# Second-norm rows and routed-tile rows: transposed by the DMA queue of SyncE instead of TensorE

## The reference

```
x = x + layernorm(attn(layernorm(x)))
x = x + layernorm(moe(layernorm(x)))

attn:  q, k, v = x @ Wqkv.T + b, 32 heads of 8;  a = q k^T;  ctx = a v      # no softmax: ctx = q (k^T v)
       group norm of ctx over (head feature, token), scaled by gn_w, gn_b;  ctx @ out_w.T + out_b
moe:   _ffn(x, gw, uw, dw) = (silu(x @ gw.T) * (x @ uw.T)) @ dw.T           # 256 -> 704 -> 256
       shared = _ffn(x, shared weights);  probs = softmax(x @ gate_w.T) over 8 experts
       the two largest probs per token, normalised, weigh the outputs of those two experts
       result = shared + sum over the two experts
```

## Time and profile before

| | us |
|---|---|
| median of 3 runs | 890.43 (889.81 to 890.58) |
| profiled execution, whole time | 889.43 |
| profiled execution, span | 887.7 |
| PE busy | 808.9 (91%) |
| DVE busy | 609.6 (69%) |
| ACT busy | 502.4 (57%) |
| POOL busy | 286.2 (32%) |

### The profile page before, as it was taken

One profiled execution on the slowest core, in us unless ns is written; L12 is line 12 of the kernel. 1 busy time (PEld: TensorE's weight loads), 2 busy tenths in 40 slices (PEclk: granted clock), 3 DMA queues, 4 the chain that ended last, 5 costly groups with the idle time before them and its releaser, 6 DMA issues.

```text
span 887.7 us, 21669 instructions
## 1 busy us (share of the span) xinstructions
PE 808.9 (91%) x6857; PEld 662.8 (75%) x6858; DVE 609.6 (69%) x1634; ACT 502.4 (57%) x1111; POOL 286.2 (32%) x316
## 2 busy tenths in 40 slices
PE   2689999999999999567999999999999999999990
PEld 1347777767777777455788989999899899999980
DVE  7556888887979797896787555555565565556562
ACT  1444748484847475523667555565656565656561
POOL 3010010101010100062354455555555454545432
PEclk9889999999999999879999999999999999999995
DMA  4104142423233323501133333334342434353523
GB/s 184 48 31 166 61 160 75 146 84 137 85 137 91 149 69 118 169 3 50 28 52 73 68 49 51 73 50 119 46 115 48 114 47 119 48 119 43 121 25 89
DMA packets 47061, 76.74 MB, mean 86 GB/s; under 512 B 8257, under 2 KB 38721, under 8 KB 45825
## 3 DMA queue, kind: packets, MB, share of 16 engines
q1 hardware_dynamic: 32016, 55.07, 18.0%
q0 software_dynamic: 14976, 20.78, 14.8%
HBM read 48.70 MB, written 27.39 MB: 86 GB/s over the span
## 4 chain that ended last, share of the span: by engine, by line
PE 82%; DVE 11%; issue 2%; DMA 2%; ACT 2%; POOL 1%; ACTq 0%; DVEq 0%; POOLq 0%
PE ps L829 41%; PE ps L844 20%; PE ps L900 5%; PE ps L935 4%; PE ps L894 3%; PE ps L988 2%; PE ps L912 2%; PE ps L920 2%; PE ps L870 1%; DVE hf L1143 1%; PE ps L905 1%; DVE wdn L1440 1%; DMA acc_d<-ysb,gst 1%; PE ps L939 1%; DVE hT L1153 1%
## 5 line engine op out<-in xcount | busy, mean ns | idle before, releaser
L829 PE MATMUL ps<-xhl,wgu 128*128 128x256 f16 x3630 | 449.3, 274 | 7.5 <-DVE hf L1143 5.9
L829 PEld LDWEIGHTS ps<-xhl,wgu 128*128 (+1 forms) x3630 | 353.2, 98 | 59.3 <-issue 7.6
L1143 DVE SCALAR_TENSOR_TENSOR hf<-ps,sc,silu 128x256 f32<-128x256 f32 x330 | 159.4, 483 | 169.6 <-ACT silu L644 132.7
L844 PE MATMUL ps<-wdn,hT 128*128 (+1 forms) x1870 | 255.0, 274 | 1.1 <-DVE hT L1153 0.7
L644 ACT ACTIVATE silu<-ps,sc 128x256 f32<-128x256 f32 x275 | 130.1, 474 | 205.8 <-PE ps L829 205.5
L844 PEld LDWEIGHTS ps<-wdn,hT 128*128 128x128 f16 x1870 | 183.0, 98 | 24.3 <-issue 1.6
L593 POOL DMA_INDIRECT acc_d<-ysb,gst x78 | 125.6, 1611 | 44.5 <-POOL gst L589 30.9
L527 POOL TENSOR_TENSOR rstd<-ve,mhalf 128x4 f32<-128x4 f32 (+1 forms) x32 | 31.1, 973 | 317.7 <-DVE ve L1329 178.6
L658 ACT CAST hT<-hf 128x256 f16<-128x256 f32 x275 | 109.6, 399 | 20.8 <-DVE hf L1143 19.5
L1153 DVE TENSOR_TENSOR hT<-hf,hT 128x256 f16<-128x256 f32 x275 | 114.7, 417 | 1.7
L582 POOL DMA_INDIRECT attw<-xn_d,gst x78 | 79.6, 1020 | 44.5 <-POOL gst L578 32.6
(11 more groups left out here) (229 smaller groups left out, 806.6 us busy)
## 6 DMA issues: line engine op xcount, KB each, us to landing
wgu<-in_gu SPq DMA_DIRECT2D x8, 1408.0 KB, 6.2
att<-in_x SPq DMA_DIRECT2D x16, 512.0 KB, 5.0
wdn<-in_dn SPq DMA_DIRECT2D x8, 768.0 KB, 8.2
x_d<-att SPq DMA_DIRECT2D x8, 512.0 KB, 2.9
xn_d<-att SPq DMA_DIRECT2D x8, 512.0 KB, 3.0
acc_d<-ysb SPq DMA_DIRECT2D x16, 256.0 KB, 3.3
att<-x_d SPq DMA_DIRECT2D x8, 512.0 KB, 4.4
att<-acc_d SPq DMA_DIRECT2D x8, 512.0 KB, 4.5
```

What stands on the lines that cost most here:

```text
L829: ins = te.matmul(o, slot_gu(slot, hw, k, j), x(hx, k), start=(n == 0), stop=(n == len(TERMS) - 1))
L844: ins = te.matmul(y_bank(u, tt), h(hh), slot_dn(slot, c, hw), start=(c == 0 and n == 0 and tt == 0), stop=(c == FC - 1 and n == 1 and tt = ...
L1143: v.scalar_tensor_tensor(out=hf[lo:P, c % 2 * TW:(c % 2 + 1) * TW], in0=up, scalar=scale_of(slot, 1, lo, P), in1=silu[lo:P, c % 2 * TW:(c ...
```

## The change

Three things are changed.

1. The second norm's rows are no longer transposed by TensorE. ACT and DVE split the rows first, as rows in SBUF (`rows2`, 128 x 4 x 2 x 256 fp16, in weight slot 7), one instruction each. Then SP issues four transposing DMAs, each of 128 rows x 512 fp16 values (hi and lo side by side) into four 128x128 blocks of `xhl`. There are now two such buffers, one in weight slot 7 for even batches and `xhl` for odd ones. The step `xhl` is gone, and `turn2` no longer takes part on TensorE. SP stores the split rows, not the fp32 rows, to `xn2_d` (the same number of bytes), behind the four transposes.
2. Since the gathered rows arrive split, the routed tiles need no split at all. SP issues two transposing DMAs for each tile, as soon as the gate and up chunks of the tile before the last are done and the rows have landed. The 4 transposes on TensorE, the ACT cast and the DVE subtraction of each tile are gone.
3. The tables `ORDER`, `START`, `LAST_ORDER` and `TAIL` are new.

The first norm's rows (`turn1`) are still transposed on TensorE.

```diff
@@ the lists: START, where it changes around turn2 @@
-         (0, "prep", 3), (0, "kv_out", 1), (0, "kv", 2), (0, "kv_out", 2), (0, "kv", 3), (0, "ln2_apply"), (0, "kv_out", 3), (0, "turn2"),
-         (0, "xhl"), (0, "state"), (0, "logits"), (0, "state_out"), (0, "logits_out")]
+         (0, "turn1_out"), (0, "q"), (0, "q_out"), (0, "kv", 0), (0, "x2"), (0, "kv_out", 0), (0, "ln2_apply"), (0, "turn2"),
+         (0, "kv", 1), (0, "kv_out", 1), (0, "kv", 2), (0, "kv_out", 2), (0, "prep", 1), (0, "kv", 3), (0, "kv_out", 3), (0, "state"),
+         (0, "state_out"), (0, "prep", 2), (0, "prep", 3), (0, "logits"), (0, "logits_out")]
...
+        spare = wgu[:, (E - 1) * SLOT_GU:E * SLOT_GU]
+        xhl_v = [a.rearrange("p (h k s) -> p h k s", h=2, k=KD) for a in (spare[:, 0:2 * KD * S], xhl[:, :])]
+        rows2 = spare[:, 2 * KD * S:2 * KD * S + 2 * NT * D].rearrange("p (t h d) -> p t h d", t=NT, h=2)
...
+            def turn2(b):
+                sp.wait_ge(rows2_made, b + 1)
+                if b > 1:
+                    sp.wait_ge(gu_done, 2 * FC * (b - 1))
+                for t in range(NT):
+                    sp.dma_start_transpose(xhl_v[b % 2].rearrange("p h k s -> p (h k) s")[:, :, t * P:(t + 1) * P],
+                                           rows2[:, t].rearrange("p h d -> p (h d)")).then_inc(x2_turned, 16)
...
-                sp.wait_ge(xn2_made, b + 1)
-                sp.dma_start(xn2_d[bass.ds(b * S, S), 0:D].rearrange("(t p) d -> p t d", p=P), xres).then_inc(xn2_stored, 16)
+                turn2(b)
+                sp.dma_start(xn2_d[bass.ds(b * S, S), 0:D].rearrange("(t p) d -> p t d", p=P),
+                             rows2.rearrange("p t h d -> p t (h d)").bitcast(F32)).then_inc(xn2_stored, 16)
...
+            def turn_x(i):
+                r = i % 2
+                sp.wait_ge(xg_loaded[r], 16 * (i + 2 - r))
+                sp.wait_ge(gu_done, FC * (2 * B + max(i - 1, 0)))
+                for t in range(TT):
+                    sp.dma_start_transpose(xt16[:, r].rearrange("p h k s -> p (h k) s")[:, :, t * P:(t + 1) * P],
+                                           xg[:, r, t, 0:D].bitcast(F16)).then_inc(xt_turned[r], 16)
...
+            for i in range(NTILE):
+                turn_x(i)
+                if i == E:
+                    sp.wait_ge(prep_lo, NSLOT * NG)
+                    sp.dma_start(x2_end, batch_rows(x2_d, B - 1)).then_inc(x2_end_loaded, 16)
+                b, n = divmod(i - E - GROUP, GROUP)
+                if b > 0 and n == 0:
+                    store_mid(b - 1)
+                if b >= 0 and n == 1:
+                    load_mid(b)
...
@@ GpSimd, gather_x @@
-                    pool.wait_ge(xg_turned, i - 1)
+                    pool.wait_ge(xt_turned[r], 16 * (i - r))
...
@@ ACT @@
-                if kind == "xhl":
-                    wait(act, gu_done, 2 * FC * b)
-                    for k in range(KD):
-                        use_done(act, b, TURN2 + k)
-                        a.activation(xhl_v[:, 0, k, :], att_bank(TURN2 + k)[:, :], ACT.Copy, scale=X_SCALE).then_inc(hi_x_made, 1)
+                if kind == "turn2":
+                    act.wait_ge(xn2_made, b + 1)
+                    wait(act, x2_turned, 16 * NT * b)
+                    wait(act, xn2_stored, 16 * b)
+                    a.activation(rows2[:, :, 0, :], xres, ACT.Copy, scale=X_SCALE).then_inc(rows2_hi, 1)
...
-            def turned_x(i, r):
-
-                act.wait_ge(xg_turned, i + 1)
-                a.activation(xt16[:, r, 0], xg_ps(r), ACT.Copy, scale=X_SCALE).then_inc(xt_hi, 1)
...
@@ PE @@
-                if kind == "turn2":
-                    turn(b, TURN2, xres, xn2_made, b + 1)
                 if kind == "logits":
-                    pe.wait_ge(xhl_made, KD * (b + 1))
+                    pe.wait_ge(x2_turned, 16 * NT * (b + 1))
...
-            def turn_x(i, r, first):
-
-                pe.wait_ge(xg_loaded[r], 16 * (i + 2 - r))
-                if not first:
-
-                    pe.wait_ge(xt_lo, i - 1)
-                for k in range(KD):
-                    for t in range(TT):
-                        ins = te.transpose(xg_ps(r)[:, k, t * P:(t + 1) * P], xg[:, r, t, k * P:(k + 1) * P], ident[:, :])
-                ins.then_inc(xg_turned, 1)
...
-                    gate_up(t, c, slot, lambda h, k: xt16[:, r, h, k, :], xt_lo, i + 1)
+                    gate_up(t, c, slot, lambda h, k: xt16[:, r, h, k, :], xt_turned[r], 16 * (i + 2 - r))
...
@@ DVE @@
-                if kind == "xhl":
-                    for k in range(KD):
-                        dve.wait_ge(hi_x_made, KD * b + k + 1)
-                        v.scalar_tensor_tensor(out=xhl_v[:, 1, k, :], in0=att_bank(TURN2 + k)[:, :], scalar=X_SCALE, in1=xhl_v[:, 0, k, :],
-                                               op0=ALU.mult, op1=ALU.subtract).then_inc(xhl_made, 1)
+                if kind == "turn2":
+                    dve.wait_ge(rows2_hi, b + 1)
+                    v.scalar_tensor_tensor(out=rows2[:, :, 1, :], in0=xres, scalar=X_SCALE, in1=rows2[:, :, 0, :], op0=ALU.mult, op1=ALU.subtract).then_inc(rows2_made, 1)
```

106 lines of the change are left out of this document (45 added, 61 removed), and 22 rows, old and new, of tables (LAST_ORDER, ORDER, TAIL).

## The result

The changed kernel takes 891.57 us (median of 20 runs, 890.02 to 893.75) against 889.79 us of the kernel before in runs beside them (20 runs, 888.42 to 890.58). The ratio is 1.0024, its 95% interval 1.0018 to 1.0031: slower by a fifth of a per cent, where 877 us was forecast. The profiled span is 889.5 us against 887.7.

The account below looks back on a forecast made before the run. TensorE was taken to bound the rounds and routed tiles, chains of waits the start and batch 7. The sum 889.4 - 16.7 - 5.3 + 4.9 + 4.0 = 876.3, plus 1.0 for the median, gave 877 us; range 868 to 911.

Parts of the forecast that it names:

- Rounds: Six like rounds: eight TensorE transposes of 0.88 us in all go from each, 5.3 us gained.
- The start: Chain from second norm to first G chunk: normalisation 1.4 us earlier, but transposing DMAs and context delay it; 4.9 us lost.
- Routed tiles: Groups of four TensorE transposes go, 38 of them between full TensorE work at 0.44 us each; 16.7 us gained.
- First routed tile: First routed G chunk starts 2.7 us later, waiting for DMAs, plus 1.3 us for a slower clock; 4.0 us lost.
- T2: Time from split's end to landing of a routed tile's two transposing DMAs: 4.9 us, under about 11.5 us of cover.
- T4: Time from split's end to landing of a batch's last of four transposing DMAs: 6.9 us, just hidden under 7.2 us.
- serial: Rival: each transposing DMA lands before the next moves, T4 11.6 us, logits wait each round; 911 us, chance 0.21.
- block: Rival: every 128x128 block holds the queue 1.0 us, T4 18.9 us, stalls in the rounds; 975 us, chance 0.09.
- fast: Rival: transposing DMAs run at plain-store pace, T4 3.0 and T2 2.0 us; start and first tile gain; 869 us, chance 0.13.
- Batch 7 and the routing: Stretch set by VectorE, whose work is the same: cost 0, with 3 us either way for new orders.
- the lists give the gain back: Rival: new order cannot hold a shorter round, 5.3 us not seen, batch 7 loses some 4; 887 us, chance 0.10.
- 40 us of room remain: Argument against the lists rival: VectorE is busy for 217.6 of 258 us in the rounds and its work is not more.

Follow-up runs that it names:

- e7_uncover: Kernel before, with the second norm's eight TensorE transposes one place earlier, ahead of the last kv group; 895.53 us, ratio 1.0071.
- e2: Changed kernel with only the rounds' list put back to the order of before; 894.79 us, ratio 1.0053.
- e3: Changed kernel with all four lists in the order of before, context of batch 1 ahead of batch 0's logits; 889.58 us, ratio 1.0000.
- e5: e1_start with the rounds' list of before, last kv group and its eviction one H step and one D chunk earlier; 901.42 us, ratio 1.0128.
- e6: e5 with the preparation's spread and scale one step earlier and its first part ahead of the state's eviction; 889.68 us, ratio 1.0000.
- e9: e6 with the logits of each batch up to the sixth moved behind the next batch's context; 887.52 us, ratio 0.9976.
- e12: e9 with VectorE's state eviction one place earlier, ahead of the first part of the weight preparation; span 883.4 us.
- e13: e12 with one more G chunk ahead of the group mean and the output projection; 921.07 us, ratio 1.0344.
- e17_after_down: Changed kernel, own lists, with the preparation's last half behind the next first norm's application and SP's residual load ahead of the staging load; 898.43 us, ratio 1.0088.
- e4_plain: Changed kernel with each transposing DMA replaced by a plain DMA of the same rows and bytes, arriving unturned; span 888.1 us.
- e11_halves: e9 with each of the second norm's transposing DMAs cut in two, eight of two blocks instead of four of four; span 911.7 us.
- e1_start: Changed kernel with the start's list in the order of before and batch 1's context ahead of batch 0's logits; 884.79 us, ratio 0.9940.

## Why the prediction was wrong

The forecast was 877 us, in a sum of -13.1 us on the profiled run; it came to +1.8, 14.9 us worse. Two steps failed, the gain in the rounds (5.8 us of the 14.9) and the cost of the start (5.7). Term by term:

- *Rounds, -5.3; measured +0.5.* This step failed in its mechanism. It took an instruction off an engine that was busy for 256.97 of 258.00 us at its full price, for "ACT and DVE keep about their work". The eight transposes did a second thing: they covered the eviction ahead of `state` (e7_uncover: 0.87 us when they are moved away, distance 43.76). Without them some 0.9 us of other cover is needed there, and in the lists that were tried the wait either stayed there (e2, e3) or came back in another place, where VectorE's chain (scale, preparation, statistics, group mean) or the transposing DMAs had no room. In the changed kernel's list they are the waits for `hf` and `hT`, 0.34 and 0.41 us and what each costs beyond its bracket. Six lists of the rounds with the transposes on DMAs and the whole preparation in place gave 43.01 us or more (the changed one, e2, e5, e6, e9, e12; e13, the mistake, 49.02). With half of the preparation out of the chain, and SP's order changed for it, a round takes 42.11. So the chain is shown as the cause in the list of e12_state. That it is the whole cause in the changed kernel's own list is not shown: there the same deferral took away the wait for `hf` alone (e17_after_down).
- *The start, +4.9; measured +10.6.* This step failed by its path. The sum let ACT's normalisation end 1.4 us earlier than before, at 63.8; it ended at 68.26, 4.5 us later than that. I had worked out what the new list does for ScalarE behind the normalisation and not what it does ahead of `turn1_out`. What follows the normalisation was sized well (8.85 us to the logits, 9.2 said). The logits are 9.17 us late, where the sum had 5.0, and 1.4 us come behind them for the lower clock, which the sum had only at the first tile. With the old order (e3_lists) the logits came 5.5 us late, the context ahead of them.
- *Routed tiles, -16.7; measured -15.8.* Right in mechanism and nearly in size. From the first routed `G` to the end -14.47 us, of which +1.32 belongs to the clock of the next term. Tiles 10.92 us, as said.
- *First routed tile, +4.0; measured +5.2.* Mechanism right, size 1.2 short: +3.88 us until the chunk starts (2.7 said) and 5.45 - 4.13 = 1.32 us for the slower clock (1.3 said). T2 was 5.9 us where 4.9 was said: issued at 427.24 and 428.53, the second landed at 433.1, 4.6 us behind its issue, beside the last shared store (issued 426.78, landed after 4.1 us, where the median of its kind is 2.2) and the next tile's two gathers. The sum had priced the pair as if alone. Turning makes up 1.1 us of it: in e4_plain the copied pair took 4.8 us at the same place.
- *T4 6.9 and its cover 7.2; no cost in the rounds.* 6.4 to 6.9 us, and 6.85 us from the split's end to the logits in the sixth round. No wait at the logits in the rounds. That the sum of T4 came so near is in part luck: the hold is 1.27 us and not 1.0, but the landing counts from the issue, so three holds stand ahead of the last landing and not four, and the landing is 2.5 us and not 2.9 (3 x 1.28 + 2.5 = 6.3). The serial, block and fast rivals fall; e11_halves shows why block by block was wrong: a DMA of four blocks costs its queue no more than one of two.
- *Batch 7 and the routing, 0 within 3.* +1.33, inside.

The sum by these terms: 9.17 + 1.40 for the start, +0.49 in the rounds, +1.33, +5.20, -15.8, together +1.8. The rival "the lists give the gain back" named the failure in the rounds, with 0.10, and its price was too small: 887 us, since it had left the start out. "40 us of room remain" on VectorE was no argument: 217.6 of 258 us is an average, and at the front of the round the engine is full.

Open: why the start's clock differs from list to list at almost the same times (the state product took 3.64 us in e3_lists, then the context 1.98; in e1_start 3.79 and 3.78), what holds the front of the changed kernel's rounds beside the preparation, and whether its own lists can be mended with a few steps.

## What to carry to other kernels

An instruction on a full engine has two prices: its own time, and the latency of others that it covers. Before taking it off, read what stands on both sides of it, and ask which eviction would be waited for if its place were empty. A low busy share of the second engine says little; what counts is its chain between the two points where the first engine meets it. And a load that waits on a late step holds everything behind it on its queue, so a deferral has to be followed through the queue that feeds it.
